# Late projections in the order key, query, value within a step, products that keep TensorE at work in the opening, and key loads on SyncE ahead of the values

## What is computed

```
x = x + attention(gn(x))          # qkv = x @ qkv_w.T + qkv_b; 7x7 mask + 16 registers
x = x + experts(gn(x))            # router top 2 of 4, fc1, gelu, weight, fc2

scores = einsum('bnqe,bnke->bnqk', q, k_cat) * scale
attn = softmax(where(mask_cat, scores, -1e30))
o = einsum('bnqk,bnke->bnqe', attn, v_cat)
out = o @ out_w.T + out_b
```

## Time and profile before

| | us |
|---|---|
| median of 3 runs | 633.26 (630.48 to 633.76) |
| the profiled execution | 633.32 |
| its span | 631.4 |
| PE busy | 557.0 (88%) |
| DVE busy | 435.6 (69%) |
| ACT busy | 312.5 (49%) |
| POOL busy | 301.4 (48%) |
| mean granted clock of TensorE | 0.966 of full speed |

### The profile page before, as it was taken

The page is one execution under the profiler, slowest core; times in us unless marked ns, Lnnn a source line. Parts: engine busy times, 40 slices in busy tenths (PEclk is TensorE's granted clock), DMA queues, the critical chain, the costliest instruction groups (busy, mean ns, idle before and its releaser), DMA issues.

```text
span 631.4 us, 22435 instructions
## 1 busy us (share of the span) xinstructions
PE 557.0 (88%) x9227; PEld 390.8 (62%) x9227; DVE 435.6 (69%) x1071; ACT 312.5 (49%) x622; POOL 301.4 (48%) x442
## 2 busy tenths in 40 slices
PE   3567969999999869999999999996988589998996
PEld 2344746767677646777677767774665346664553
DVE  6784559887976658678977898668795558763332
ACT  1762534447767624444444444556664438744321
POOL 4105746885387712556579713465554232313221
PEclk8697989999999979999999999999899799999999
DMA  9858979566866598756876588666520011211122
GB/s 309 194 140 218 277 238 219 172 174 156 198 182 167 164 320 202 206 152 182 203 186 184 156 205 210 161 175 193 128 61 6 2 38 38 77 41 54 57 76 75
DMA packets 130988, 97.79 MB, mean 155 GB/s; under 512 B 66684, under 2 KB 123944, under 8 KB 130888
## 3 DMA queue, kind: packets, MB, share of 16 engines
q1 hardware_dynamic: 120456, 73.84, 44.6%
q0 software_dynamic: 10432, 22.52, 11.5%
HBM read 59.83 MB, written 35.68 MB: 151 GB/s over the span
## 4 chain that ended last, share of the span: by engine, by line
PE 62%; DVE 17%; DMA 6%; issue 5%; POOL 4%; ACT 3%; SPq 2%; DVEq 0%; POOLq 0%; ACTq 0%
PE ps L1177 41%; PE ps L1309 5%; PE ps L1328 5%; PE ps L1331 4%; PE ps L1279 3%; DMA QS<-MT 3%; DVE MX L609 2%; DVE ST L511 2%; DVE KU L579 1%; DVE XH L603 1%; DMA X<-in_x 1%; DVE GT_ L549 1%; DVE KT L588 1%; PE ps L1294 1%; PE ps L1450 1%
## 5 line engine op out<-in xcount | busy, mean ns | idle before, releaser
L984 ACT ACTIVATE PT<-ps 128x448 f32<-128x448 f32 (+1 forms) x207 | 96.2, 508 | 99.0 <-PE ps L1309 98.8
L609 DVE TENSOR_REDUCE MX<-ps 128x2 f32<-128x372 f32 x216 | 106.8, 535 | 14.0 <-PE ps L1279 13.9
L1177 PE MATMUL ps<-X,WQ 128*128 128x384 f16 x486 | 89.8, 333 | 2.5 <-POOL X L377 1.6
L491 POOL TENSOR_TENSOR KT<-QS,KT 128x384 f16<-128x384 f32 x36 | 34.3, 961 | 94.6 <-ACT KT L1094 94.6
L1328 PE MATMUL ps<-PT,VR 128*32 128x112 f32 (+1 forms) x1656 | 76.6, 259 | 0.0
L1177 PE MATMUL ps<-OS,WO 128*128 128x384 f16 x324 | 70.2, 327 | 5.9 <-POOL OS L419 3.7
L1331 PE MATMUL ps<-PT,SELW 128*32 128x112 f32 (+1 forms) x1656 | 74.0, 253 | 0.0
L1177 PE MATMUL ps<-XH,WQ 128*128 128x384 f16 x324 | 62.4, 342 | 8.6 <-DVE XH L559 7.9
L1309 PE MATMUL ps<-QS,KB 122*128 122x112 f16 (+1 forms) x864 | 59.4, 213 | 11.5 <-DMA QS<-MT 11.2
L1177 PEld LDWEIGHTS ps<-X,WQ 128*128 128x128 f16 x486 | 46.1, 100 | 30.8 <-issue 4.3
L1279 PE MATMUL ps<-KB,QS 120*32 120x186 f16 x1728 | 56.8, 246 | 8.5 <-DMA QS<-qscr 5.2
(11 more groups left out here) (182 smaller groups left out, 1068.3 us busy)
## 6 DMA issues: line engine op xcount, KB each, us to landing
KB<-kscr SPq DMA_DIRECT2D x108, 192.0 KB, 3.8
kscr<-KT SPq DMA_DIRECT2D x36, 384.0 KB, 5.1
VR<-vscr SPq DMA_DIRECT2D x216, 56.0 KB
QS<-qscr SPq DMA_DIRECT2D x108, 96.0 KB, 3.9
qscr<-QT POOLq DMA_DIRECT2D x36, 192.0 KB, 3.7
X<-in_x SPq DMA_DIRECT2D x6, 576.0 KB, 7.0
vscr<-VT POOLq DMA_DIRECT2D x54, 64.0 KB, 2.4
vscr<-WR POOLq DMA_DIRECT2D x54, 64.0 KB, 2.7
```

Of the source, the lines that this page charges most:

```text
L491: nc.gpsimd.tensor_tensor(HW[:, m % 2, 1, k, :], HF[:, unit % 2, :], HW[:, m % 2, 0, k, :], ALU.subtract).then_inc(s_["hl"], 1)
L609: V.tensor_reduce(out=MX[:, g % 2, t, 2 * pair:2 * pair + 2], in_=ps[:, S_BANK(i), 0:2 * RUN].rearrange("p (h n) -> p h n", h=2), op=ALU.m ...
L984: A(PTS[pt_slot(n)][:, 0:w], ps[:, ST_BANK(n), 0:w], ACT.Exp, scale=SCORE).then_inc(s_["exd"], 1)
L1177: last = mm(bank, lhsT(a, k), rhs(b, k), start=(k == 0 and n == 0), stop=(finish and k == steps - 1 and n == 2))
```

## The change

The late units get a fixed place in a step: `fillers(g, p)` gives a key strip for p = 0, a query for p = 1 and a value for p = 2; steps 9 to 11 have no key strip, and steps 12 to 14 have a second one, in p = 2. Key strips are made three steps earlier than before, values and queries within their own stage's steps, so that steps 30 to 32 still have five units. Before the loop there are 16 units instead of 18, over six banks. The normalisation of image 0 moves two of its three low halves from VectorE to POOL and the third value from ScalarE to VectorE. TensorE runs products whose result nobody reads ahead of the first key strips (14) and after five of them (8 each). The registers' and the bias products come before the first scores. SP loads queries and keys ahead of the values. The loads of the second image are spread over steps 0 to 2 and 15 to 17, each after the step's maxima. `register_keys` moves from third 0 of step 3 of a stage to third 2 of step 2. The clearing of `CS[0]` on POOL moves ahead of the last low half. The weights of the router and the experts are split two steps later, and the logits of the router are taken in steps 33 to 35.

```diff
+LAG = 32
+def fillers(g, p):
+    gi, s = divmod(g, TILES)
+    out = []
+    if p == 0 and gi == 2 and s < 3:
+        out.append((3, "k", 2 * s))
+    elif p == 0 and (gi, s) not in ((1, 3), (1, 4), (1, 5)):
+        out.append((gi + 1 + (s + 3) // TILES, "k", (s + 3) % TILES))
+    if p == 1:
+        out.append((gi + (s + 4) // TILES, "q", (s + 4) % TILES))
+    if p == 2:
+        out.append((gi + (s + 3) // TILES, "v", (s + 3) % TILES))
+        if gi == 2 and s < 3:
+            out.append((3, "k", 2 * s + 1))
+    return [u for u in out if u[0] < STAGES]
+FIRST = tuple((0, "k", i) for i in range(STRIPS)) + ((0, "q", 0), (0, "q", 1), (0, "v", 0), (0, "q", 2), (0, "v", 1), (0, "q", 3))
+BESIDE = ((0, "v", 2), (1, "k", 0), (1, "k", 1), (1, "k", 2))
+BANK_OF = {u: (4, 6, 2, 3, 5, 7)[f % 6] if f < 16 else 6 for f, u in enumerate(UNITS)}
-POOL_K = ((), (0, 1, 2), (0, 1, 2), ())
+POOL_K = ((0, 1), (0, 1, 2), (0, 1, 2), ())
...
             for g in range(LAST):
+                if g + 3 < LAST:
+                    queries_in(g + 3)
+                    keys_in(g + 3)
                 if g + 1 < LAST:
                     values_in(g + 1)
-                if g + 3 < LAST:
-                    keys_in(g + 3)
-                    queries_in(g + 3)
...
-                    if p == 0 and gi + 2 < STAGES and s == 3:
+                    if p == 2 and gi + 2 < STAGES and s == 2:
                         register_keys(gi + 2)
...
                     if p == 1 and g + 1 < LAST:
                         maxima_in(g + 1)
+                    if g < KC and p:
+                        at = (p - 1) * 3 * SN
+                        pool.dma_start(raw1(g, at, 3 * SN), x[1, :, g, at:at + 3 * SN]).then_inc(x_in[1][g][p - 1], 16)
+                    if 15 <= g < 18 and p:
+                        i = 2 * (g - 15) + p - 1
+                        if i == 0:
+                            pool.wait_ge(s_["v_mm"], 6 * KC)
+                        at = i % 2 * 3 * SN
+                        pool.dma_start(xs(1, i // 2, at, 3 * SN), x[1, :, i // 2, at:at + 3 * SN]).then_inc(x_re[i], 16)
...
+            pool.wait_ge(s_["st_mm"], 36 * STAGES)
+            nc.gpsimd.memset(CS[0], 0.0).then_inc(s_["csz"], 1)
             low_output(LAST - 1)
...
             for a in range(STRIPS):
-                for k in range(2):
+                for k in range(KC):
                     normalised(0, a, k)
-                if a == 0:
-                    weights_low(0)
-                for k in range(KC):
-                    low_half(0, a, k)
+                low_half(0, a, 2)
...
-                        if (s, p) == (1, 1):
+                        if (s, p) == (3, 1):
                             moe_weights_low(1, rwraw, RWs)
-                        if (s, p) == (2, 0):
+                        if (s, p) == (4, 1):
                             moe_weights_low(2, wr_flat, W1)
-                        if (s, p) == (2, 2):
+                        if (s, p) == (4, 2):
                             moe_weights_low(3, f2raw, W2)
...
+            def keep_busy(count):
+                for i in range(count):
+                    mm(ps[0:LEAD, 1, 0:HEADS * LEAD], KB[0:96, 0, 0, 0:LEAD], KB[0:96, :, 0, 0:LEAD], start=True, stop=True)
+            keep_busy(14)
+            for f, u in enumerate(FIRST):
+                unit(*u)
+                if f < STRIPS - 1:
+                    keep_busy(8)
+            for g in (1, 2):
+                registers(g, 2 - g)
+            pe.wait_ge(*evicted(0, "q", 1))
+            value_bias()
...
+            pe.wait_ge(s_["obx"], 1)
+            for p in range(3):
+                scores(0, 2 * p)
+                scores(0, 2 * p + 1)
+                unit(*BESIDE[p])
...
-                    if gi < STAGES - 1:
-                        if g == 0 and p == 0:
-                            pe.wait_ge(s_["obx"], 1)
-                        unit(gi + 1, *NEXT[s][p])
+                    for u in fillers(g, p):
+                        unit(*u)
```

More of the change, by code:

```diff
@@ L1226, in values @@
             def values(gi, s):
-                pe.wait_ge(*bank_before(gi, "v", s))
-                if gi == 0 and s == TILES - 1:
-                    pe.wait_ge(s_["t_ev"], 1)
+                for before in bank_before(gi, "v", s):
+                    pe.wait_ge(*before)
+                if gi == KC:
+                    second_image(s)
                 for b in range(KC):
@@ L1406, in _ @@
                     else:
-                        if p == 1 and s:
-                            logits(0, s - 1)
+                        if p == 1:
+                            for blk in {LAST - 3: (0, 1), LAST - 2: (2, 3), LAST - 1: (4,)}.get(g, ()):
+                                logits(0, blk)
                         if n > LAG * STRIPS:
```

283 lines of the change are left out of this document (123 added, 160 removed).

## The result

| | before | after |
|---|---|---|
| median, us | 632.19 (4 runs) | 653.66 (650.92 to 655.5, 4 runs) |
| ratio | | 1.0325, 95% interval 1.0294 to 1.0355 |
| span of the profiled execution | 631.4 | 652.3 |
| PE busy | 557.0 | 572.4 |
| mean granted clock | 0.966 | 0.961 |

The change makes the kernel slower by 21 us. I had forecast 615.0 with 603 to 628 as range; the time lies beyond it, on the side to which I had given 0.07. Ratios leave out executions over 1.5% slower than the fastest of their kernel: one of ten in E1, three in E2 and eight in E7, in the last two the profiled one among them.

The account below looks back on a forecast made before the run. TensorE was taken to bound steps 0 to 29. Loop start 63.7, loop 346.7, steps 30 to 35 54.35 + 0.5, the rest (631.4 - 481.00) - 2.6 make 613.1 of span, plus 1.9 outside: 615.0 us, range 603 to 628.

Parts of the forecast that it names:

- Opening, strips: Key strips before the loop: 3.15 us a strip instead of 3.49, last strip starting at 37.9, 2.0 earlier.
- Opening, after the strips: Last strip to first score product unchanged at 14.0 us, then 11.8 to the loop, which starts at 63.7.
- Both stalls go: TensorE's waits for the maxima's rows at 87.23 and 233.22 us vanish, worth 6.9 and some 7.5 us.
- stall 1: TensorE's 5.25 us wait for the maxima's rows at 87.23, 6.9 us with the slow restart, forecast to go.
- (a) POOL waits for a key store: POOL's wait before copying registers' keys delays TensorE: 6.2 us from step 14, 2.0 from step 2, 0.5 each from 8, 20.
- Slower: Rival, chance 0.07: POOL's wait for key stores costs in all four stages, 26 us more, 641.
- (b) The image's loads: Second image's loads cost 2.5 us in steps 0 to 2 and 1.5 in steps 15 to 17.
- Transfers and the port: Rival, chance 0.15, 625 us: strips at 3.9 (+3.8), 3 us more in steps 0 to 2 and 15 to 17.
- (c): Steps 12 to 14: two units in one third share bank 6, the second waits, 3 x 0.6 us.
- (d): Steps 9 to 11: two units take 9.5 us and ScalarE already works 8.5 a step, costing 1.0.
- Key loads ahead of the values at nothing: SyncE's loads in the loop: keys only go earlier, values start no later than their own wait allows; no cost.
- Steps 30 to 35 and router: Steps 30 to 35 take 0.5 us more, VectorE bounding; the router gains 2.6.

Follow-up runs that it names:

- E1: Changed kernel with only the place of `register_keys` undone, back to the first third of a stage's fourth step: 631.62 us, ratio 0.9998 to the kernel before.
- E2: Changed kernel with SyncE issuing the key store of a step's first third ahead of the next step's value loads: 638.25 us, ratio 1.0085.
- E7: E1 with the second image's six first loads all in step 0 again: ratio 0.996 from two executions.
- E3: Changed kernel with all low halves of the first normalisation on VectorE, none on POOL: 646.97 us, ratio 1.024.
- E8: E1 without the extra products that keep TensorE at work in the opening: 636.6 us, ratio 1.0047.
- E14: E5 with four of the second image's six first loads in the opening and the last two in step 2: 622.71 us, ratio 0.9826.
- E13: E1 with the second image's second read cut to 96 of 1152 columns, so its output isn't the reference's: 628.25 us, ratio 0.9931.
- E9: E5 with value projected second and query last in each step, queue order keys, key store, values, queries: 640.82 us, ratio 1.0148.
- E12: Changed kernel with value projected second and query last, SyncE's queue as keys, values, queries: 639.96 us, ratio 1.0135.
- E4: Changed kernel with SyncE's old order of loads, values, then keys, then queries: 693.01 us, ratio 1.1003.
- E5: Changed kernel with E1, E2 and E3 together, and the router weights' low part ahead of VectorE's other work in step 33: 629.27 us, ratio 0.9938.
- E6: E5 with the second image read again in six steps instead of three: 630.14 us, ratio 0.9949.
- E10: E9 with the experts' weights converted a third of a step later on ScalarE and VectorE: 641.44 us, ratio 1.0159.
- E11: E10 with the second image read again in six steps instead of three: 634.07 us, ratio 1.0039.
- B1: Kernel before with four of the second image's six first loads in the opening and the last two in step 2: 632.76 us, ratio 1.0004.

## Why the prediction was wrong

Against the span of 652.3, my sum of 613.1 is short by 39.2: 5.3 in the opening, 26.3 in steps 0 to 29, 7.6 behind them.

*What bounds the kernel now* stands: the regular step is set by TensorE, before and after (10.95 to 11.03 before, 10.99 after).

*Opening, strips: the term mis-sized.* 3.15 us a strip was VectorE's own sum with POOL "beside that"; it is 3.80 on the mean, which makes the last strip 3.4 late (41.29 against 37.9). The slow low half adds 0.5 us a strip and the slow third block 0.6. The rule that I quoted from the Trainium skill (SBUF — State Buffer, Who interferes with whom) and then set aside fits the first of these: VectorE's low half reads two SBUF inputs and took twice its time beside POOL's, and E3 shows it free of that. The block reads one SBUF input of that size, so the sentence that I quoted doesn't cover it. By that rule of the Trainium skill I had put the strip near 3.9 us and the opening 3.8 longer, close to what came. My own sum for VectorE was not too low: E3's 3.71 with three low halves, less two at 0.5 each, is 2.7 against my 3.1.

*Opening, after the strips.* 14.4 us to the first scores, 14.0 forecast. From there to the loop 13.4, 11.8 forecast: the 1.3 that I gave back for a clock that stays high wasn't there, since TensorE idled 1.42 before the first score and was granted 0.63 in 56 to 60. The added products hold the clock during the strips, but the loop starts no later without them (E8).

*Both stalls go*: right, no wait on the maxima's rows over 1.0 us. But the gain at stall 1 was no gain. It had been a wait beside full queues, and with the loads spread out a wait as long stood in step 2. I had priced this at 2.5 us; steps 0 to 3 show 50.06 (before), 50.3 (E1), 50.0 (E7, all in step 0), and 44.45 in E14.

*(a) POOL waits for a key store: the step that failed.* For step 15 I had 6.2 us, and it is 5.1, by the chain that I described (idle 3.38, forecast 3.3 to 5.5). For steps 3, 9 and 21 I took 2.0, 0.5 and 0.5; they are 5.7, 6.7 and 4.6 (changed kernel less E1). I wrote that the strip "is made in the first third and lands near 9 to 12 us, just at the need", counting from when it is ready. In E2 it is issued 4.5 us into the step, but I didn't follow it through SyncE's queue, where `values_in(g + 1)` stands ahead of it and waits for a value store. In the kernel before, value tiles were made two to four steps ahead of their load, so nothing of the kind stood there. The sum over the four is 22.1 instead of 9.2. The rival "Slower" had the mechanism and its place right, priced it at 26 more, and named the landing from which it decides (10 us into the step; it is 15.3 in step 8, 19.0 in step 2 and 13.3 in step 20). The transfer itself was not slow, 5.0 us in step 8: the time goes in the queue ahead of it. What I held against it, that such landings belong to the stretches with image loads, was wrong: step 8 has none.

*(b) The image's loads*: 4.0 forecast. Step 2 is 4.8 over the regular step and step 17 5.3. E13 shows the bytes as the cause in 15 to 18. The two are 6.1 more than forecast. With the strips' 3.4 that is the rival "Transfers and the port" at nearly its price (3.8, and its 625 takes 3 for each of the two stretches), and it came on top of "Slower". I read the cost so: a value tile made in the last third is loaded just when it is wanted, which the prediction never asked about values. E9 and E12 fit that from the other side: give the value a third more, and the query stalls.

*(c), (d).* The shared bank: the last thirds of steps 12 to 14 are 5.82 against 3.60 and 1.46 for the second unit, 0.76 each, 2.3 in all (1.8 forecast). Steps 9 to 11 without their stall are 10.4 each where I had 9.5 and 1.0 in all for ScalarE: 1.7 more. Together (a) to (d) make 21.2 of the 26.3 by which steps 0 to 29 are over my sum; the other 5.1 I can't assign.

*Key loads ahead of the values at nothing*: they cost nothing, but it isn't an edit with one answer. E4 puts 40 us on it. My cover, that keys "only go earlier", was true, and it missed that with late units the old order would have been ruinous.

*Steps 30 to 35 and router*: 2.1 less forecast, 5.5 more measured. The first logits still wait for the router's weights on VectorE, longer than in the earlier trace rows, and the experts' conversions stand in VectorE's chain a little later. VectorE's wait for POOL of the earlier trace rows did go: its last normalisation and the router follow at once.

```profile
479.74 0.19 PE L1373 MATMUL ps<-WQ,X 128*128 128x8 f16 x1 [4.04 <-DVE WQ L592]
...
492.84 1.83 DVE L592 SCALAR_TENSOR_TENSOR WQ<-WR,WQ 128x1152 f16<-128x1152 f32 x1
...
495.52 2.05 DVE L592 SCALAR_TENSOR_TENSOR WQ<-KT,WQ 128x1152 f16<-128x1152 f32 x1
...
508.09 0.56 DVE L656 TENSOR_TENSOR ON<-ps,RINV 128x384 f32<-128x384 f32 x1
508.56 0.22 DVE L792 SCALAR_TENSOR_TENSOR QS<-ps,SM 128x72 f32<-128x72 f32 x1
```

I had moved the weights' load away from the need but not looked at VectorE's list in step 33, where five operations, from 476.65 us on, run ahead of it (it starts at 479.05); in E5, where it goes first, that third takes 4.66 us instead of 8.53. The 2.3 us behind the router go with a lower granted clock (0.84 in the 20 us from 514.75, the router's end, against 0.89 from 495.43 before); no run isolates that.

*What stays open*: why E8 loses 0.5%, what decides whether the stall of the first steps falls in step 1, 2 or 3 and that of the second read in step 16, 17 or 18, the 5.1 us of steps 0 to 29, the rest of E3's gain, and the 2.3 us behind the router.

## What to carry to other kernels

When units are made later, list for each result every queue between its making and its use, and for each queue what stands ahead and what that waits for; a transfer is late by the latest of these, not by its own readiness. A wait added on an in-order engine costs what stands behind it: put it behind the work that the bound engine wants next (E1, one line, 21 us). Bytes that fill the queues cost about the same here when they were spread differently within a full stretch (E1 and E7, E5 and E6; but E10 and E11 differ by 1.2%). A stretch with room took them for nothing (E14), and the time fell only where the rest of the schedule could use it (B1).

## What the hardware showed

VectorE's subtraction of two SBUF inputs took 1.08 us beside POOL's and 0.55 alone. Of its blocks, which scale and shift one such input, the one that started beside POOL's operation took 1.07 and the others 0.47. So giving two of three low halves to POOL made VectorE slower than keeping all three (4.09 against 3.71 us a strip). With the six first loads of 576 KB in steps 0 to 2, where DMA engines were busy 0.93 of the time, steps 0 to 3 took 50.3 us, and 44.45 with four of them in the opening (E5, E14). There they cost nothing that showed, where the share went from 0.64 to 1.01. A high share by itself was thus no sign of a cost: what mattered, as I read it, is whether a chain with no slack ran beside it.
